# Openings of four stages reordered, and two steps of the rotary loop moved, in a decoder of eight layers

## The reference

```python
x = x + tanh(g_xattn[0]) * _L0_xattn_ref(_layernorm(x), ...)   # long convolution
x = x + tanh(g_ffn[0])   * _L0_ffn_ref(_layernorm(x), ...)     # 32 experts
x = x + tanh(g_xattn[1]) * _L1_xattn_ref(_layernorm(x), ...)   # cross attention, mask, layer norm
x = x + tanh(g_ffn[1])   * _L1_ffn_ref(_layernorm(x), ...)     # top-1 gate picks a shared head
x = x + tanh(g_xattn[2]) * _L2_xattn_ref(_layernorm(x), ...)   # rotary attention, 16 heads of 128
x = x + tanh(g_ffn[2])   * _L2_ffn_ref(_layernorm(x), ...)     # bit-linear: 8-bit rows, ternary weights
x = x + tanh(g_xattn[3]) * _L3_xattn_ref(_layernorm(x), ...)   # cross attention, 8-bit weights and rows
x = x + tanh(g_ffn[3])   * _L3_ffn_ref(_layernorm(x), ...)     # shared and routed experts
```

## Time and profile before

| | |
|---|---|
| median of three executions | 2554.68 us |
| the profiled execution | 2560.05 us |
| its span | 2558.0 us |
| mean granted TensorE clock | 0.942 of full speed |

### The profile page before, as it was taken

The page is one execution under the profiler, slowest core; times in us unless marked ns, Lnnn a source line. Parts: engine busy times, 40 slices in busy tenths (PEclk is TensorE's granted clock), DMA queues, the critical chain, the costliest instruction groups (busy, mean ns, idle before and its releaser), DMA issues. The chain is left out here.

```text
span 2558.0 us, 38354 instructions
## 1 busy us (share of the span) xinstructions
PE 2190.7 (86%) x10438; PEld 1386.8 (54%) x10486; DVE 1518.7 (59%) x3734; ACT 1139.1 (45%) x3571; POOL 686.8 (27%) x892
## 2 busy tenths in 40 slices
PE   6969999986888588868998999899986588869999
PEld 3446687754555344425555555555553344436685
DVE  6965434455555477745676677667765567762244
ACT  2021244411555255535555556555553367742242
POOL 5615500163233100013333333333332000002204
PEclk9959999998999799989999999999997689989999
DMA  6902245455000000000000000000000000020143
GB/s 234 276 18 89 94 146 162 128 162 198 1 0 0 3 1 0 0 25 1 1 1 1 0 0 0 0 0 0 0 0 1 4 5 5 20 85 35 55 139 99
DMA packets 85588, 127.19 MB, mean 50 GB/s; under 512 B 12418, under 2 KB 74626, under 8 KB 84226
## 3 DMA queue, kind: packets, MB, share of 16 engines
q1 hardware_dynamic: 75490, 98.52, 12.0%
q0 software_dynamic: 9984, 27.28, 3.4%
HBM read 91.41 MB, written 47.84 MB: 54 GB/s over the span
## 5 line engine op out<-in xcount | busy, mean ns | idle before, releaser
L2280 ACT ACTIVATE l2x_prob<-l2x_pS,l2x_nb,l2x_rms_q 128x256 f32<-128x256 f32 x256 | 142.4, 565 | 119.0 <-DVE l2x_nb L2507 117.3
L1031 ACT ACTIVATE moe_act_g<-moe_pG 128x96 f32<-128x96 f32 (+1 forms) x159 | 53.2, 335 | 267.1 <-PE moe_pU L964 186.7
L1179 PE MATMUL l2x_pQ<-big,l2x_xT 128*128 128x512 f32 x320 | 153.7, 603 | 7.0 <-DVE l2x_part L2485 6.5
L2504 DVE TENSOR_REDUCE l2x_negmax<-l2x_pS 128x2 f32<-128x512 f32 x128 | 87.8, 686 | 116.1 <-PE l2x_pS L2102 113.4
L2112 PE MATMUL l2x_pOT<-l2x_probT,l2x_v 128*128 128x512 f32 x256 | 125.4, 612 | 21.5 <-ACT l2x_probT L2295 21.5
L3013 DVE TENSOR_TENSOR l3f_hid<-l3f_act_g,l3f_pA 128x256 f32<-128x256 f32 (+1 forms) x103 | 38.2, 371 | 159.3 <-ACT l3f_act_g L2924 127.0
L2102 PE MATMUL l2x_pS<-l2x_kT,l2x_qT 128*128 128x256 f32 x512 | 130.0, 384 | 0.0
L924 POOL DMA_INDIRECT moe_yk<-route_y,moe_slot_i x72 | 70.2, 975 | 220.1 <-DMA route_y<-moe_y 188.1
L2837 PE MATMUL l3f_pA<-big,l3f_xnT 128*128 128x512 f32 x256 | 125.2, 613 | 0.0
L2261 ACT ACTIVATE l2x_square<-l2x_pQ 128x128 bf16<-128x128 f32 x384 | 101.7, 294 | 48.8 <-PE l2x_pQ L1179 48.8
L2121 PE MATMUL l2x_pT<-big,l2x_oT 128*128 128x256 f32 x512 | 121.1, 380 | 0.7 <-ACT l2x_oT L2288 0.7
(11 more groups left out here) (481 smaller groups left out, 5793.8 us busy)
## 6 DMA issues: line engine op xcount, KB each, us to landing
route_x<-in_c_zero SPq DMA_DIRECT2D x1, 13184.0 KB, 79.6
moe_xg<-route_x SPq DMA_DIRECT2D x103, 128.0 KB, 2.1
route_y<-moe_y SPq DMA_DIRECT2D x103, 128.0 KB, 1.7
big<-in_e_gu SPq DMA_DIRECT2D x1, 6144.0 KB, 18.4
l3f_xg<-route_x SPq DMA_DIRECT2D x39, 128.0 KB, 2.2
route_y<-l3f_y SPq DMA_DIRECT2D x39, 128.0 KB, 1.7
big<-in_f_gu SPq DMA_DIRECT2D x1, 4096.0 KB, 12.2
big<-in_e_down SPq DMA_DIRECT2D x1, 3072.0 KB, 24.7
```

The costliest lines, as they stand in the source:

```text
L1179: last = pe.matmul(out, lhsT=xT[:, k, :], rhs=w[:, k, cols], start=(k == 0), stop=(k == KC - 1))
L2280: ins = act.activation(prob[g % 2][:, h, :], pS[j][:, (h % 2) * 2 * P:(h % 2 + 1) * 2 * P], ACT.Exp, scale=rms_q[g][:, h:h + 1], bias=nb[: ...
L2504: dve.tensor_reduce(negmax[:, c], pS[j][:].rearrange("p (h k) -> p h k", h=2), AX.X, ALU.max, negate=True).then_inc(S["max_steps"], 1)
```

## The change

Six things are done, in `Ternary`, `Turned` and four stages.

- The three attention stages: the clears move from VectorE to GpSimd, the row and value tiles behind batch 0's `stats`, the `blocks` behind batch 1's. VectorE's `rows` of batch 0 waits for the first, ScalarE's first copy for the second (`blank`).
- `phase_l1_attention`: mask, biases and scales are prepared ahead of batch 1's statistics.
- `phase_l1_ffn`: the lane sums' product follows batch 0's `xT`, their addition batch 0's `normalise`, the second product batch 0's projections, and the means stand ahead of the step `ternary`, whose lag goes from 0 to 1. The bank is `pO` in place of `pT`.
- `phase_l3_attention`: both weights are rounded ahead of batch 1's statistics, the first one's products stand in batch 0's `qk`, the second one's behind its `v`; the second is read behind batch 1's `quantX`. The rounding loses its two clips and a copy, `scale_cols` becomes two tiles wide, and both weights go through `pO`.
- `phase_l2`, opening: statistics first, then the tables. The first four units of batch 0 go to four banks, and TensorE's, ScalarE's and VectorE's `prepare0` take the third ahead of the first turn.
- `phase_l2`, loop: `f_quant_h` goes from ScalarE to GpSimd, where it heads step 0. In step 3 TensorE takes `turn_probs(..., 1)` ahead of `output`.

The diff, cut to its core:

```diff
@@ Turned
-    def clear(self, dve):
-        for t in self.blocks:
-            dve.memset(t[:], 0.0)
-        dve.memset(self.q[:], 0.0)
-        dve.memset(self.k[:], 0.0).then_inc(self.rows_ready, 1)
-        dve.wait_ge(self.rows_ready, 1)
+    def clear_rows(self, pool):
+        pool.memset(self.q[:], 0.0)
+        pool.memset(self.k[:], 0.0).then_inc(self.rows_ready, 1)
+
+    def clear_blocks(self, pool):
         for t in self.blocks:
+            pool.memset(t[:], 0.0).then_inc(self.blank, 1)
...
     def scalar(self, act, b, p):
         act.wait_ge(self.turned_ps, b + 1)
+        if isinstance(b, int) and b == 0:
+            act.wait_ge(self.blank, 2)
@@ phase_l1_attention, and alike in the two others
             def stats(b, p):
                 nm.pool(pool, b, p)
...
                 pool.tensor_copy(cT[p][:], G["ctxT"][:, :, bass.ds(b * P, P)]).then_inc(cT_ready, 1)
+                if isinstance(b, int) and b == 0:
+                    tq.clear_rows(pool)
+                    clear_values()
+                if isinstance(b, int) and b == 1:
+                    tq.clear_blocks(pool)
...
+            def stats_of(b, p):
+                if isinstance(b, int) and b == 1:
+                    constants()
+                nm.vector(dve, b, p)
@@ phase_l1_ffn
-                 ("S2", 2), ("P1", 2), ("V0", 2), ("turn", 1), ("back", 3), ("normalise", 0), ("ternary", 0),
+                 ("S2", 2), ("P1", 2), ("V0", 2), ("turn", 1), ("back", 3), ("normalise", 0), ("ternary", 1),
...
+            def ternary_part(b, p):
+                if isinstance(b, int) and b == 0:
+                    dve.wait_ge(*G["loaded"]["l2f"])
+                    ternary.means(dve)
+                ternary.vector(dve, b, p)
@@ phase_l3_attention
+            def weights(j):
+                pe.wait_ge(wsteps, 8 * j + 8)
+                after(pe, w_read, 2 * j)
...
                 project(pe, pQK[:, C:2 * C], cT[p], W["L3_wk"])
+                if isinstance(b, int) and b == 0:
+                    weights(0)
+                    pe.wait_ge(w_read, 2)
...
                 for k in range(KC):
-                    ch(dve.tensor_scalar(wrows[:, k, :], w[:, k, :], winv[:, k:k + 1], 127.0, ALU.mult, ALU.min))
-                    ch(dve.tensor_scalar(wrows[:, k, :], wrows[:, k, :], -127.0, ROUND, ALU.max, ALU.add))
-                    ch(dve.tensor_scalar(wq8[:, k, :], wrows[:, k, :], -ROUND, None, ALU.add))
-                ch(dve.tensor_copy(winv[:], wamax[:]))
+                    ch(dve.tensor_scalar(wrows[:, k, :], w[:, k, :], winv[:, k:k + 1], ROUND, ALU.mult, ALU.add))
+                ch(dve.tensor_scalar(wq8[:], wrows[:], -ROUND, None, ALU.add))
...
+            def stats_of(b, p):
+                if isinstance(b, int) and b == 1:
+                    dve.wait_ge(*G["loaded"]["small"])
+                    quantise_weights(0, "q")
+                    read_weights(0, "q")
+                    quantise_weights(1, "o")
+                nm.vector(dve, b, p)
@@ phase_l2
+        def bank(b, u):
+            return (pQ, pP, pF, pS[1])[u] if isinstance(b, int) and b == 0 and u < 4 else pQ
...
                 proj(0, 0, 1)
+                proj(0, 0, 2)
                 trans(0, 0, 0)
+                proj(0, 0, 3)
                 value_rows(0, 0, 1)
-                proj(0, 0, 2)
                 trans(0, 0, 1)
-                proj(0, 0, 3)
                 trans(0, 0, 2)
...
+                if g == 3:
+                    turn_probs(*before(b, p, g, 1), 1)
                 if at_least(b, g, 2):
...
                     output(*before(b, p, g, 2))
-                if at_least(b, g, 1):
+                if g < 3 and at_least(b, g, 1):
                     turn_probs(*before(b, p, g, 1), 1)
...
-            def f_quant_h(c):
-                act.wait_ge(F["qh_steps"], 4 * c + 4)
-                after(act, F["hq_ps"], c)
-                act.activation(f_qh_q[:], f_val, ACT.Copy, bias=-ROUND).then_inc(F["qh_ready"], 1)
...
+            def f_quant_h(c):
+                after(pool, F["hq_ps"], c)
+                hold(pool, F["qh_steps"], 4 * c + 4, spare)
+                pool.tensor_scalar(f_qh_q[:], f_val, -ROUND, None, ALU.add).then_inc(F["qh_ready"], 1)
```

230 lines of the change are left out of this document (142 added, 88 removed).

## The result

The changed kernel takes 2490.92 us (median; 2480.97 to 2500.33), the kernel before on the same chip 2557.06 us: ratio 0.9745, 95% interval 0.9718 to 0.9772, so 66 us less. 2484 us had been predicted, between 2475 and 2500. The profiled execution took 2485.77 us (span 2483.6), against 2560.05 (span 2558.0) before: 74.3 us less.

A forecast was written before the change was run, and what follows sets the result against it. Outside the heavy loops the path is a chain of waits, TensorE being 86% busy. 10.2 + 7.3 + 17.4 + 14.0 + 22.2 - 0.3 = 70.8 us off 2560.05 gives 2489.3; against the median 2484, range 2475 to 2500.

The forecast's parts named there:

- The sum: Whole kernel: the gains of the four openings and the loop, less the tail's cost, come to 70.8 us.
- First attention stage, 10.2: First attention stage's opening: earlier statistics, with clears on GpSimd, gain 10.2 us, between 8 and 10.6.
- Shared-head stage, 7.3: Shared-head stage's opening: statistics move from 859.31 to 851.95, gaining 7.3 us, between 6.5 and 7.5.
- Rotary opening, 17.4: Rotary stage's opening: statistics 6.5, first product to first scores 9.4, first maximum 1.6; 17.4 us gained, range 11 to 18.5.
- Last attention stage, 14.0: Last attention stage's opening: earlier statistics, weights' quantisation moved behind batch 0's; 14.0 us gained at ScalarE's copy, released by GpSimd's clear.
- The loop, 22.2: Rotary loop: rounding on GpSimd removes TensorE's whole wait, 12 x 1.715 + 1.63 = 22.2 us, GpSimd's instruction taking 1.0 to 2.5.
- The tail, -0.3: Rotary stage's tail: the last two roundings are on the path and cost 0.3 us on GpSimd, up to 3.
- The fourth step's order, 0: Rotary loop's fourth step: second turn ahead of output product only moves the wait; gain 0, loss up to 0.1 a batch.
- A: Openings give less: clears twice as long, held two-input VectorE instructions, or low clock in the rotary opening; 2495 us, chance 0.19.
- B: Rotary loop keeps its period, as another chain holds TensorE; all 22 us lost, 2506 us, chance 0.11.
- D: Stages' barriers: shorter openings are given back where a clock or load comes later; 2554 us, chance 0.02.
- C: Rotary loop: a long GpSimd rounding holds VectorE's line 2507 to its end; slower from 7.9 us on, chance 0.02.

The follow-up runs named there:

- the repeat: The changed kernel's same program run once more on another chip, against the kernel before: 2489.11 us, ratio 0.9753.
- the third order of the step: Changed kernel, fourth step: output product first again, ScalarE's second probabilities copy ahead of squares, VectorE's scaling ahead of multiplications; ratio to the kernel before 0.9702.

## Why the prediction was right, point by point

- **The sum.** 70.8 us were predicted, 66 came. The difference of the profiled pair, 74.3, is nearer to 70.8 only by its clocks. By the means above, 65.2, the sum was 5.6 us too high: 2.3 in the first attention stage, 1.4 in the shared-head stage, 0.4 in the last attention stage and 1.5 in the rotary stage, where by the repeat's trace the tail cost 3.2 us more than said and the last batch 0.6, and opening and loop gave 2.4 more.
- **First attention stage, 10.2.** 9.0 us by the first scores, 8.9 in the trace, 7.9 in the mean of all. The statistics moved as said. The prices of the clears were right, and the sentence "if a clear also holds VectorE's instructions meanwhile, one more is lost" named what came; the loss is 2.0 us (all clears moved), not one, and I had taken a value near its absence.
- **Shared-head stage, 7.3.** 10.6 in the pair, but 6.6 to 7.3 between traces whose clock rose at the same batch (258.3 against 251.1 to 251.8, 254.9 against 247.6 and 247.8). The term was right, or a little high; 3.5 us are the clock.
- **Rotary opening, 17.4 and the first wait of 1.7.** 19.9 together. The statistics gave 6.6, from the first product to the first scores 8.7 came where 9.4 stood, since the second product still ran partly at the low clock (2.92 us where 1.95 was taken), and the first maximum gave 1.6 as said. Another 1.2 came in the steps behind it, which no term had: in the 20 us behind the first maximum the granted clock was 0.91 before and is 1.00 after. The 11 us that the run with one bank shows are measured in the new order, and aren't the 9.4 of the sum, which start from the old one.
- **Last attention stage, 14.0.** 13.2 at ScalarE's copy, released by the clear as said; 12.7 at the scores. The step that was short is the same as in the first stage: held normalisations, worth 2.6 us. The other 6.2 us of the pair's 18.9 lie in batches 3 to 7 and are the clock's.
- **The loop, 22.2.** The waits went in full: 1.77 us a batch. The price behind it was wrong. The GpSimd instruction costs 2.78 us, not 1.0 to 1.6, since a copy's time was taken for an addition's; that the "at most 2.5" and the estimate of 0.9 us beside it fail as well is the same step. The slack covered it: 3.0 us remain ahead of TensorE's turn, and doubled it costs 0.08 us a batch. That it holds VectorE for no longer than a copy does was luck: the prediction had allowed for a hold to the end of at most 2.5 us.
- **The tail, -0.3, "up to -3".** -3.9. This is the mis-sized term that counts: the same instruction, twice, with nothing beside it (3.0 us from VectorE's scaling to TensorE's turn, against 1.14).
- **The fourth step's order, 0.** 0.00 to 0.01 us a batch, with the wait at its new place, and 0.6 us once in the last batch, where the table's -0.7 comes from. The reason given, ScalarE's unchanged order between the two copies, agrees with what the third order of the step gained.
- **Rivals.** A (the openings give less) came in part, by one of its three causes: held VectorE instructions, of the kinds with one input and not two, and the clears weren't dear. B and D didn't come. C's mechanism is refuted for the rounding: line 2606 isn't held by it, and a second one of 2.78 us behind it costs 0.08 us a batch.

## What to carry to other kernels

Price an instruction that goes to another engine by that instruction on that engine. A copy of the same width isn't one, and where the row is missing, ask at each of its places what covers twice the guess: here the loop did and the tail didn't. Work given to an idle GpSimd isn't free while VectorE runs instructions of the kinds that it holds; put it where VectorE reads PSUM, reduces or waits. And when an order is changed to kill a wait, change it on the engine whose queue makes the waiter late.

## What the hardware showed beyond that

- GpSimd adds a constant to 1024 f32 columns in 2.77 us and copies or casts them in 1.04, whatever the output's type; it adds two tiles of 1024 in 2.34 and clears 2048 in 1.80.
- What GpSimd holds on VectorE depends on both instructions (table above), and the addition of a constant holds for about 0.9 of its 2.77 us.
- One VectorE instruction can be held by several of GpSimd's in a row: 2.34 and 2.31 us across four clears, 3.06 across two. When VectorE's short instructions came during the clears (small clears moved), they got in between, one for each clear. Why the first didn't is open.
- The same program has its TensorE clock at 1.00 in one execution and at 0.80 in another for the same batches of the last attention stage, and the two traces differ by 5.9 us in that stage and by 4.0 in the shared-head stage. A single pair of traces can't tell such a gain from a change's; the times of equal batches, read together with the granted clock, can. What decides when the clock rises wasn't tested.
